# Layer 0 of a two-layer transformer kernel: states read as a strided matmul operand, the feed-forward spread over two trips in another split

## The reference, cut to what matters

```
h = GRU(initial_state=cond, inputs=x)                  # 32 steps, one after the other; all 64 sequences at once
q, k, v = h @ Wq.T, h @ Wk.T, h @ Wv.T                 # 16 heads of 128
q, k = rmsnorm(q) * gq, rmsnorm(k) * gk
x = x + softmax(causal(q k^T / sqrt(128))) v @ Wo.T    # the attention sum, x1 in the kernel
y = depthwise_causal_conv(x, taps=cond) + b            # 32 taps
y = int8_round(y)
g = silu(y @ gate.T) * (y @ up.T)                      # gate, up, down: weights rounded to -1, 0, 1
x = x + int8_round(rmsnorm(g) * ln) @ down.T           # the feed-forward sum, x2
```

## Time and profile before

| | |
|---|---|
| median of 3 runs | 1751.12 us (1750.25 to 1754.61) |
| the profiled execution's own time | 1748.3 us |
| its span, first to last instruction | 1746.1 us |
| mean granted TensorE clock | 0.916 of 2.4 GHz |
| PE busy / DVE busy / ACT busy / POOL busy | 1473.6 / 1126.3 / 860.5 / 459.6 us |

### The profile page before, as it was taken

How to read it: one execution, slowest core, us unless ns; L and a number is a source line. 1 busy time by engine, 2 the same in 40 slices (tenths; PEclk the granted TensorE clock), 3 DMA queues, 4 the chain that set the end, 5 groups by cost and what they waited for, 6 DMA issues and landing times.

```text
span 1746.1 us, 25621 instructions
## 1 busy us (share of the span) xinstructions
PE 1473.6 (84%) x8515; PEld 1141.9 (65%) x8530; DVE 1126.3 (65%) x2635; ACT 860.5 (49%) x1740; POOL 459.6 (26%) x337
## 2 busy tenths in 40 slices
PE   7999999787979797979888857397798988989897
PEld 6677776456867575757676745265585766757676
DVE  3999998924355455464646464764967668686684
ACT  4676677556555555555564642443433343343311
POOL 3766666511222313131313121000010110101102
PEclk8989989898989898998999978698899999999999
DMA  8122222240010010100000041000000000000000
GB/s 343 37 54 55 49 78 55 79 145 25 31 41 21 25 36 24 36 24 31 29 30 30 31 166 55 6 19 13 1 13 7 13 19 6 13 6 7 13 7 12
DMA packets 25006, 73.58 MB, mean 42 GB/s; under 512 B 4052, under 2 KB 4566, under 8 KB 23384
## 3 DMA queue, kind: packets, MB, share of 16 engines
q1 hardware_dynamic: 23640, 65.77, 12.0%
q10 hardware_dynamic: 1280, 6.75, 1.0%
HBM read 49.43 MB, written 23.07 MB: 42 GB/s over the span
## 4 chain that ended last, share of the span: by engine, by line
PE 59%; DVE 21%; issue 10%; ACT 7%; POOL 2%; DMA 1%; DVEq 0%; POOLq 0%; SPq 0%; ACTq 0%
PE psum L551 11%; PE psum L866 7%; PE psum L837 6%; PE psum L655 6%; PE psum L487 3%; PE psum L596 3%; PE psum L583 3%; PE psum L876 3%; PE psum L502 2%; DVE work L1711 2%; ACT probs_t L1381 2%; PE psum L563 2%; PE psum L783 1%; PE psum L479 1%; DVE work L1780 1%
## 5 line engine op out<-in xcount | busy, mean ns | idle before, releaser
L551 PE MATMUL psum<-work,w_big 128*128 128x256 f32 x1024 | 258.9, 400 | 48.9 <-POOL work L1546 37.8
L551 PEld LDWEIGHTS psum<-work,w_big 128*128 128x128 f32 x1024 | 195.8, 199 | 87.9 <-issue 49.7
L1711 DVE SCALAR_TENSOR_TENSOR work<-work,h_all 128x248 f32<-128x248 f32 (+30 forms) x558 | 156.3, 359 | 0.2 <-DVE work L1711 0.2
L866 PE MATMUL psum<-w_big 128*128 128x256 f32 x512 | 133.1, 420 | 23.3 <-ACT w_big L1410 23.3
L866 PEld LDWEIGHTS psum<-w_big 128*128 128x128 f32 x512 | 107.1, 213 | 49.6 <-ACT w_big L1410 31.4
L487 PEld LDWEIGHTS psum<-gru_mem 128*128 128x128 f32 x768 | 102.4, 215 | 42.1 <-DVE gru_mem L1811 32.6
L1611 POOL TENSOR_TENSOR stats<-stats,minus_half 128x32 f32<-128x32 f32 x16 | 94.6, 5912 | 133.4 <-ACT stats L1163 133.4
L487 PE MATMUL psum<-gru_mem 128*128 128x128 f32 x768 | 104.5, 299 | 25.5 <-DVE gru_mem L1811 25.4
L502 PE MATMUL psum<-w_big,h_all 128*128 128x512 f32 x256 | 121.2, 618 | 5.6 <-ACT w_emb L1083 5.6
L655 PE MATMUL psum<-w_big,gru_mem 128*128 128x256 f32 x512 | 123.1, 403 | 0.0
L1546 POOL COPY work<-h_all 128x256 f32 (+1 forms) x16 | 71.8, 4513 | 188.5 <-PE psum L551 188.5
(11 more groups left out here) (264 smaller groups left out, 2992.0 us busy)
## 6 DMA issues: line engine op xcount, KB each, us to landing
value_rows<-w_emb SPq DMA_DIRECT2D x128, 128.0 KB, 2.3
work<-value_rows SPq DMA_DIRECT2D x16, 1024.0 KB, 5.6
x_res<-out SPq DMA_DIRECT2D x15, 256.0 KB, 2.8
work<-in_w SPq DMA_DIRECT2D x1, 2048.0 KB, 11.4
w_big<-in_Wv SPq DMA_DIRECT2D x1, 2048.0 KB, 16.2
w_big<-in_Wq SPq DMA_DIRECT2D x1, 2048.0 KB, 18.4
w_big<-in_Wk SPq DMA_DIRECT2D x1, 2048.0 KB, 21.2
w_big<-in_Wo SPq DMA_DIRECT2D x1, 2048.0 KB, 24.9
```

The costliest lines, as they stand in the source:

```text
L551: mm = pe.matmul(bank(n % 2)[:, o * TA:(o + 1) * TA], w_big[:, s, k * H * HD + at:k * H * HD + at + HD], hc[:, k, :], start=(k == 0), stop ...
L866: mm = pe.matmul(bank(2 + g)[:, 0:D], o1_t[:, h, g * P:(g + 1) * P], wo1[:, h, :], start=(h == 0), stop=(h == H - 1), skip_group_check=True)
L1711: ins = dve.scalar_tensor_tensor(dst[:, :, lag:], src[:, :, :T - lag], tap, dst[:, :, lag:], ALU.mult, ALU.add)
```

## The change

Three things are done. First, `hc`, `chunk_in` and the semaphore `hc_on` go: the q/k tiles take `h_all` itself as the moving operand, with a view that steps over sequences and times. Two elements that follow each other in this view lie 64 floats (256 bytes) apart. Second, the feed-forward of a chunk is split elsewhere. Before, `gate_up` 0 and 1 and the rounding of group 0 were in trip i and the rest in trip i+1. Now only `gate_up` 0 (and its `silu`) is in trip i; `gate_up` 1, 2, 3 and the rounding of both groups are in trip i+1. With that, `turn_yq` is moved behind `outputs(2i+1)`, and the calls of the first half of a trip stand in another order on TensorE, VectorE and ScalarE. Third, `add_ffn` writes its sum to a second buffer `x2` (in a free piece of `w_big`), which SP stores, in place of writing over `x1`; the attention sum of the next chunk then waits for `x2_on`, not for the store.

```
-        hc = work[:, 0:512].rearrange("p (k n) -> p k n", k=KD)
+        x2 = w_big[:, 2, 2048:2560].rearrange("p (g n) -> p g n", g=GA)
...
@@ TensorE: qk_tiles @@
-                            mm = pe.matmul(bank(n % 2)[:, o * TA:(o + 1) * TA],
-                                           w_big[:, s, k * H * HD + at:k * H * HD + at + HD], hc[:, k, :],
+                            mm = pe.matmul(bank(n % 2)[:, o * TA:(o + 1) * TA].rearrange("p (b t) -> p b t", t=T),
+                                           w_big[:, s, k * H * HD + at:k * H * HD + at + HD],
+                                           h_all[:, k, 1:T + 1, bass.ds(i * BA, BA)].rearrange("p t b -> p b t"),
...
@@ TensorE: chunk, first half of a trip @@
                 if tail:
-                    gate_up(c - 1, 2)
+                    gate_up(c - 1, 1)
                 scores(2 * i, 1, first)
                 qk_tiles(i, 1, (1,))
                 scores(2 * i, 2, first)
                 if tail:
-                    gate_up(c - 1, 3)
+                    gate_up(c - 1, 2)
                 qk_tiles(i, 1, (2,))
                 square_sums(2 * i + 1, 0)
                 scores(2 * i, 3, first)
                 if tail:
-                    down_turn(c - 1, 0)
+                    gate_up(c - 1, 3)
                 qk_tiles(i, 1, (3,))
-                if tail:
-                    down(c - 1, 0)
-                    down_turn(c - 1, 1)
                 if ffn:
...
                     residual(c, (0,))
                 if tail:
-                    down(c - 1, 1)
+                    down_turn(c - 1, 0)
+                qk_tiles(i, 1, (4,))
+                if tail:
+                    down(c - 1, 0)
                 if ffn:
                     residual(c, (1,))
-                qk_tiles(i, 1, (4,))
+                if tail:
+                    down_turn(c - 1, 1)
+                qk_tiles(i, 1, (5,))
+                if tail:
+                    down(c - 1, 1)
                 square_sums(2 * i + 1, 1)
-                qk_tiles(i, 1, (5,))
+                qk_tiles(i, 1, (6,))
                 if ffn:
                     turn_x1(c)
-                qk_tiles(i, 1, (6,))
...
@@ TensorE: chunk, second half @@
-                        if n == 0:
-                            pe.wait_ge(hc_on.sem, KD * i + 2 * KD)
...
@@ ScalarE: chunk, second half @@
                 exps(2 * i + 1)
+                if more:
+                    keep_qk(2 * i + 2, (6,))
+                spread_probs(2 * i + 1)
+                if more:
+                    keep_qk(2 * i + 2, (7,))
+                keep_outputs(2 * i + 1, 1, range(PAIRS))
+                if more:
+                    keep_sums(2 * i + 2)
                 if ffn:
                     keep_yq(c)
-                if more:
-                    keep_qk(2 * i + 2, (6, 7))
-                spread_probs(2 * i + 1)
-                if ffn:
                     silu(c, 0)
...
@@ VectorE: chunk @@
                 if tail:
-                    hidden(c - 1, 1, (0, 1))
-                    weigh(c - 1, 1)
-                    quantise_hidden(c - 1, 1, lambda ins: link(ins, hid_step, c - 1))
-                    hid_step.end_trip()
+                    hidden(c - 1, 0, (0, 1))
+                    weigh(c - 1, 0)
+                    quantise_hidden(c - 1, 0, tail_link)
+                    hidden(c - 1, 1, (0,))
                 soft_in(2 * i)
                 if tail:
-                    add_ffn(c - 1, 0)
+                    hidden(c - 1, 1, (1,))
+                    weigh(c - 1, 1)
                 soft_out(2 * i)
                 if tail:
+                    quantise_hidden(c - 1, 1, tail_link)
+                    hid_step.end_trip()
+                    add_ffn(c - 1, 0)
                     add_ffn(c - 1, 1)
...
                 soft_in(2 * i + 1)
+                soft_out(2 * i + 1)
                 if ffn:
                     quantise_y(c, flink)
-                soft_out(2 * i + 1)
-                if ffn:
-                    hidden(c, 0, (0, 1))
-                    weigh(c, 0)
-                    quantise_hidden(c, 0, flink)
...
@@ ScalarE: chunk, first half (its silu and hidden_squares follow TensorE's new order) @@
...
@@ GpSimd: chunk_in is gone; hidden_rms of both groups stands in the next trip @@
```

More of the change, by code:

```diff
@@ L1250, in chunk @@
                 if tail:
-                    silu(c - 1, 2)
+                    silu(c - 1, 1)
                 take_scores(2 * i, 1)
                 keep_qk(2 * i + 1, (1,))
+                if tail:
+                    hidden_squares(c - 1, 0)
                 take_scores(2 * i, 2)
                 if tail:
-                    silu(c - 1, 3)
+                    silu(c - 1, 2)
                 keep_qk(2 * i + 1, (2,))
@@ L1259, in chunk @@
                 if tail:
-                    hidden_squares(c - 1, 1)
-                    keep_hidden(c - 1, 0)
+                    silu(c - 1, 3)
                 keep_qk(2 * i + 1, (3,))
                 if tail:
+                    hidden_squares(c - 1, 1)
+                exps(2 * i)
+                if tail:
+                    keep_hidden(c - 1, 0)
+                keep_qk(2 * i + 1, (4,))
+                spread_probs(2 * i)
+                if tail:
                     keep_hidden(c - 1, 1)
-                exps(2 * i)
-                spread_probs(2 * i)
-                keep_qk(2 * i + 1, (4, 5))
+                keep_qk(2 * i + 1, (5, 6))
                 if ffn:
                     keep_x1(c)
-                keep_qk(2 * i + 1, (6, 7))
+                keep_qk(2 * i + 1, (7,))
                 if first:
@@ L1304, in chunk @@
                     silu(c, 1)
[L1305 to L1310, removed]
                     hidden_squares(c, 0)
-                if not more:
                     silu(c, 2)
@@ L1559, in recurrence @@
                         .then_inc(h_kept.sem, 1)
-                    if step == 3 and last:
-                        pool.wait_ge(h_kept.sem, T + 1)
-                        pool.wait_ge(w5_out, 16)
-                        chunk_in(0)
                     if step >= 2:
@@ L1619, in chunk @@
                 if tail:
+                    hidden_rms(i - 2, 0)
                     hidden_rms(i - 2, 1)
-                if more:
-                    pool.wait_ge(proj_sum.sem, (2 * i + 2) * TILES)
-                    chunk_in(i + 1)
                 head_rms(2 * i + 1)
-                if ffn:
+                if not more:
                     hidden_rms(i - 1, 0)
-                if not more:
                     row_rms(0)
@@ L1943, in add_ffn @@
                 dve.wait_ge(down_sum.sem, GA * c + g + 1)
-                dve.scalar_tensor_tensor(x1[:, g, :], bank(7)[:, 0:D], h_as[g], x1[:, g, :], ALU.mult, ALU.add)\
+                if g == 0 and not (isinstance(c, int) and c == 0):
+                    dve.wait_ge(x2_out, 16 * c)
+                dve.scalar_tensor_tensor(x2[:, g, :], bank(7)[:, 0:D], h_as[g], x1[:, g, :], ALU.mult, ALU.add)\
                     .then_inc(x2_on.sem, 1)
@@ L1979, in chunk, with hlink @@
                 soft_in(2 * i + 1)
+                soft_out(2 * i + 1)
                 if ffn:
                     quantise_y(c, flink)
[L1982 to L1983 removed]
+                    ffn_step.end_trip()
+                if not more:
+                    def hlink(ins):
+                        link(ins, hid_step, c)
                     hidden(c, 0, (0, 1))
                     weigh(c, 0)
[L1986 to L1988 removed]
+                    quantise_hidden(c, 0, hlink)
                     hidden(c, 1, (0, 1))
@@ L2187, in _ @@
             chunk(1, False, True, True)
-            with dve.Fori(0, NA - 3) as last:
-                chunk(last + 2, True, True, True)
+            chunk(2, True, True, True)
+            with dve.Fori(0, NA - 4) as last:
+                chunk(last + 3, True, True, True)
             chunk(NA - 1, True, True, False)
```

47 lines of the change are left out of this document (18 added, 29 removed).

## The result

The changed kernel takes 1838.95 us (median of 4 runs, 1837.71 to 1839.53), the kernel before 1750.68 beside it: a ratio of 1.0499 [1.0481, 1.0517], slower by 88 us. The forecast was 1675, faster. Rival 1, the strided reading, named 1848 to 1877 and had a chance of 0.30.

A forecast was written before the change was run, and what follows sets the result against it. TensorE's list was taken as the chain, lengthened by waits of 17.8 us a trip. Winning 13.0 a trip, 78 in six, less 2, gives 76 us: 1675 from 1751.1; own range 1655 to 1695, full range 1655 to 1870.

The forecast's parts named there:

- Rival 1: Every q/k tile: the strided reading slows the matmul, 1848 to 1877 us; chance 0.30 in full, 0.07 in small form.
- the strided operand: q/k tiles, 1024 records: strided reading taken to cost zero, since bf16 rows on TensorE showed spare element rate; range up to 202 us.
- The bound from VectorE's hops: Upper bound for q/k tiles from VectorE's strided reduce: 0.77 ns an element, 198 ns a record, 202 us in all.
- What the slower tiles hid: If strided reading slowed the q/k tiles, they would hide up to 4.8 x 6 = 29 us of the new waits.
- The sum without that term: Waits of 17.8 us a trip less new ones leave 13.0; six trips 78 us, less 2 at layer end: 76.
- the copy with its wait: First q/k tile behind GpSimd's copy: removal wins 6.3 us wait plus 2.4 slow clock, 8.7 a trip in six trips.
- `gate_up` 0: Feed-forward, right behind `turn_yq`: new wait of 0.9 us a trip for ScalarE's copy and two hand-overs.
- `gate_up` 3: First half of a trip: new wait of about 1.6 us for bank 7, emptied by VectorE's `hidden` behind the rounding.
- small ones: First half of a trip, dense on ScalarE and VectorE: 1 us a trip put down for small new waits.
- the outputs: TensorE's wait at `outputs(2i+1)`: falls from 2.9 to 1.3 us a trip, with no fall of the clock priced behind it.
- The convolution's margin: VectorE's convolution against the scores: its 10.1 us of slack shrinks until it is late by some 0.4 us.
- Rival 2: Waits come back elsewhere, at `outputs` and `gate_up` 3: 1699 us, or 1723 if the clock falls again; chance 0.11.

The follow-up runs named there:

- e5: Separate kernel computing nothing of the reference: streams of 256-column matmuls differing in operand layout; float32 took 0.85 ns an element for neighbours, 1.70 at step 64.
- e6: Changed kernel with states stored as pairs of steps side by side, q/k tiles reading runs of two floats, whole reference computed: 1667.38 us, 0.9537 of before.
- e1: Changed kernel with q/k tiles reading 256 neighbouring floats (wrong tokens, output not the reference's): 1666.11 us, 0.9539 of before.
- e4: Kernel before, old order, without the copy and its wait, q/k tiles reading neighbouring floats (output not the reference's): 1698.64 us, 0.9701 of before.
- e10: e6 with GpSimd's power over 32 means taken in two instructions of 16, those of k first: 1660.91 us, 0.9479 of before.
- e8: Kernel before with x1's transposes and ScalarE's copy of them, which starts the convolution, moved one q/k tile later: 1724.56 us, 0.9854 of before.
- e9: e3 with x1's transposes and ScalarE's copy of them moved one q/k tile earlier, where before has them: 1723.04 us, 0.9835 of before.
- e3: Changed kernel with the copy (`hc`, `chunk_in`, `hc_on`) put back, new order and second buffer kept: 1680.5 us, 0.9592 of before.

## Why the prediction was wrong, point by point

**The step that failed** is the choice in the strided operand: "I take zero, because TensorE's own row is nearer than VectorE's." The bf16 row shows that the array can be fed an element in 0.50 ns or less when eight elements share a 16-byte line. It says nothing of the rate of lines, and a float32 view of step 64 needs a line for every element. e5 measures that rate, 1.70 ns, against 0.85 for the array. The bound from VectorE's hops, 0.77 ns an element and 202 us, was within a tenth: measured are 0.85 ns, 218 ns a record and 1024 x 218 = 223 us. VectorE's row was the right witness in kind, since each of its elements was in a line of its own, which the bf16 row's weren't. That its size fitted so well is luck: another VectorE instruction in e5 pays (380 - 290) / 256 = 0.35 ns an element for the same 32-byte step, and 0.58 for 256 bytes.

**What the slower tiles hid.** The view costs 173 us in the end, not 223, so 50 came back. e6 shows most of where: its waits at the outputs and at `gate_up` come to 17.7 + 6.9 + 5.9 = 30.5 us in six trips, less the 3.8 that the changed kernel still has, and the clock behind the outputs to 6 x 1.6 = 10, together 37. The trips agree: 128 records are 27.9 us more a trip, and a trip went from 77.2 to 98.5, so 6.6 were hidden, 40 in six. The last 10 weren't traced. The prediction had put it at up to 29, since it priced no clock there. So 1675 + 223 - 50 = 1848, less the 9 by which the rest of the sum was too high (below), is the measured 1839, 9 under the 1848 to 1877 of rival 1.

**The sum without that term** was 76 us and gives 1675; e1 measured 1666 and e6, with the true tokens, 1667. The trips are the forecast 77 us (GpSimd's L1603 stands at 516.88 and, five trips on, at 902.69 in e6: 77.2), and the copy with its wait is 52 (e4). But the terms fit less well than their sum. New waits a trip: `gate_up` 0 0.9 forecast, 0.98 measured; `gate_up` 3 1.6 and 1.15; small ones 1.0 and none; the outputs 1.3 and 2.95, with a fallen clock that had been priced at nothing. The outputs' miss is GpSimd's power, which in the new order falls into the convolution: VectorE starts `soft_in` 1.8 us later for it, and 1.3 + 1.8 = 3.1. The walk over VectorE's and ScalarE's lists left GpSimd's out. e10 took 1.0 us off that wait and only 0.3 off the outputs', since the exps come right behind; so this share is worked out, not shown by a run. What made up for it can be read in four trips of before and five of e6:

```profile
564.81:926.34 361.53, 305.21 (x1787) 245.60 (x1794) 188.11 (x477) 195.66 (x405) 96.08 (x24) 0.92 0.09 29
```

```profile
516.88:902.69 385.81, 360.00 (x2231) 293.28 (x2241) 230.13 (x596) 245.12 (x506) 77.72 (x22) 0.97 0.11 34
```

Idle time falls from 14.1 to 5.2 us a trip, 8.9 where the sum has 13.9 - 4.8 = 9.1: the small waits that never came paid for the outputs. Busy time falls from 76.3 to 72.0, 4.3 where 3.9 of clock were priced, although e6 still loses 1.6 at the outputs: the clock had cost more in before than at the two places where the prediction priced it. That these misses cancel is luck.

**The convolution's margin** was read rightly: 0.4 us late forecast, 0.5 in e6. And e8 shows what one tile later costs without the rest of the new order: half of what the copy gives, lost again at `turn_yq`.

**Rival 2** (waits that come back elsewhere) was right in kind in e6 and e8, but didn't decide.

**What the copy was.** "The copy stays visible for its whole 11 us on GpSimd because it runs while VectorE does the convolution" holds for a start 2.5 us or more behind the convolution's first instruction (before, e9), not for 0.85 us (e3, e8). So even with the copy kept, the new order is worth 71 us (e3): 29 with a slow copy (e9, where `turn_x1` stands as in before) and 43 by making it a fast one. In the new order, then, taking the copy out gives some 10 to 13 us more (e6 against e3), not 52.

## What to carry to other kernels

Price a strided operand by the 16-byte lines that it touches, at about 1.7 ns a line, and take as a witness only a row whose elements lie in lines as yours do; if it comes out too dear, store the data so that two float32 or four bf16 of a line are read in a row, which was free here (L69, L82). A second engine's short instruction beside another's dense stretch can take seven times as long or not, by a microsecond of its start: before removing it, try to move it. When a stall is removed, walk the lists of all engines, the idle one too, since its slow instruction may be next.

## What the runs showed of the hardware

- **The line rate isn't tied to the data type**: 256 elements from 256 lines took 34.84 / 80 = 436 ns in float32 (L65, clock 1.00) and 17.42 / 40 = 436 in bf16 (L79, clock 0.50).
- **At the lower clock the hop is hidden in float32.** Behind idle time, 10 records of the step of 64 took 4.68 us and 10 of neighbours 4.63, at granted clocks of 0.58 and 0.50 (timeline, then stretches, e5):

```profile
616.21 4.68 PE L90 MATMUL psum<-big,wts 128*128 128x256 f32 x10 [5.48 <-DVE dst L108]
642.39 4.63 PE L93 MATMUL psum<-big,wts 128*128 128x256 f32 x10 [21.50 <-DVE dst L115]
```

```profile
616.00:621.00 5.00, 4.68 (x10) 2.98 (x10) 0.23 (x2) 0.00 (x0) 0.00 (x0) 0.58 0.00 0
642.00:647.00 5.00, 4.61 (x10) 3.20 (x10) 0.34 (x1) 4.63 (x11) 0.00 (x0) 0.50 0.00 0
```

- **The stationary operand pays too**: loading 128 columns of float32 took 192 ns for neighbours and 313 at a step of 64, and 80 records of 128 columns took 17.76 us in place of 9.10. ScalarE, VectorE and GpSimd went from 406, 290 and 402 ns for 256 neighbours to 643, 438 and 615 at a step of 64.
- **GpSimd beside VectorE's convolution** is either let in at once or held for some 9 to 10 us more. The Trainium skill (SBUF — State Buffer, "Who interferes with whom") says that the two share a pair of ports, which whoever starts first holds for its whole instruction. The fast copy agrees in part: a convolution instruction beside it took 0.84 us, its neighbours 0.47. Why a start 1.6 us later is held for many such instructions in a row, and is let in before the convolution ends, stays open.
